# Layer 1 of a two-layer perceiver: the turn of the second rows between the products of q, k and of v, and a later start of the output bias

## The chip, the cores and the metric

The kernel runs on one core of one Trainium2 chip, all in float32. The metric is the device time of one execution in microseconds (us). TensorE (PE in the profile) multiplies, VectorE (DVE), ScalarE (ACT) and GpSimd (POOL) do the rest, SyncE (SP) issues the transfers. Each engine runs its own list of instructions in the written order; semaphores tie the lists together.

## The reference, cut to what matters

The input x has 64 batches of 32 rows of 512 values. Six blocks follow each other, each of the form x = x + f(layernorm(x)). Layer 0 has a cross attention, a self attention and a feed-forward step with adapters. Layer 1, the only part that the change touches, has these three:

```
x = x + mix(layernorm(x))                  # blend of crucial and other channels, gates from a convolution
h = layernorm(x);  q, k, v = split(h @ w_qkv.T + b_qkv)
p = softmax(where(causal, k q^T, -10000))  # 8 heads of 32
x = x + (p^T v) @ w_o.T + b_o              # b_o: the output bias
x = x + layernorm(x) @ (W * mask).T        # feed-forward
```

## The kernel before, in words

The 2048 rows are cut into 16 tiles of 128 rows (four batches each). Layer 1 takes every tile t through a list of stages. The ones that matter here, in the order of one tile:

- gate, add_rest, mix (DVE, lines 1809, 1816, 1822), turn_mix (four transposes on PE, line 1704), add_mix (DVE, line 1826: x = x + the turned mix).
- stats1, rstd1, rows1: the first norm. DVE takes the statistics (lines 1074 to 1079), POOL the power (line 1084), DVE writes the normalised rows to lane_xn (line 1089). turn1 transposes them on PE (line 1105), ACT copies the result to lane_xnT (line 1771).
- qkv on PE: 16 products of 128x128 for q and k (line 1716), then 4 products 128x256 for v (line 1720). ACT stores q and k (line 1778), DVE stores v (evac_v, line 1846), POOL spreads k over the batches (spread_k, line 1676).
- scores (PE, line 1728), mask (DVE, lines 1852 to 1857), shift (POOL, line 1684), exps (ACT, line 1783), turn_probs (DVE, lines 1863 to 1871), spread_p (ACT, line 1791), values (PE, line 1743), evac_ot (ACT, line 1797), project (PE, line 1751).
- bias (POOL, line 1671) adds b_o to x once rows1 of the tile has read x; add_proj (DVE, line 1876) adds the projection after it.
- stats2, rstd2, rows2, turn2, xnT2: the second norm, through the same helper lines as the first (1074 to 1105), so that line 1089 is rows1 or rows2, and line 1105 is turn1 or turn2.
- ffn (PE, line 1757), add_ffn (DVE, line 1880), store (SP).

Below, a number behind a stage is its tile: turn2(0) is the turn of tile 0's second rows.

Four tiles are under way at once, one in each of four lanes of buffers (t % 4). What an engine does in which order is set by a table: SLOTS1 gives every stage a time, in units of a tile's period, and over_lanes (line 1130 on) sorts all pairs of tile and stage by the tile's start plus the stage's slot. This is done three times: for an opening, with the starts of tiles 0 to 7 given in STARTS1 (0.00, 0.45, 0.99, 1.56, 3.50, 4.58, 5.35, 6.53); for a loop that runs twice and does four tiles each time, with starts one apart; and for a closing, with starts for tiles 12 to 15 (0.00, 37.47, 38.83, 39.38). The sort is the order of issue, no more: an engine comes to an instruction when all before it on this engine are issued, and waits there for its semaphores. On PE such a wait holds all products behind it.

Two waits are not obvious from the list. turn_mix(t) waits until add_ffn(t-4) has freed the lane. In places where PE would be idle for long, keep_busy (line 1518) puts products of a matrix of ones; in the closing there are seven of them (14 records of the trace) directly ahead of values(15).

Of the kernel before, what the change touches and what calls it, by code (L numbers as in the profile page):

```python
# [19 lines left out]
NT = B // TB  # L20
# [24 lines left out]
LANES = 4  # L45
# [1019 lines left out]
def norm_sems(sem, name):  # L1065

    return {k: sem(f"{name}_{k}") for k in ("stats", "veps", "rstd", "xn", "xt", "xnT")}
# [14 lines left out]
def norm_rstd(pool, n, t, u, small, neghalf):  # L1082
    pool.wait_ge(n["veps"], t + 1)
    pool.tensor_tensor(small["rstd"][:, u], small["veps"][:, u], neghalf[:], ALU.pow).then_inc(n["rstd"], 1)  # L1084
# [17 lines left out]
def norm_turn(pe, n, t, u, xn, out, ident):  # L1102
# [16 lines left out]
    "reduce_rest": 3.994,}  # L1119
SLOTS1 = {  # L1120
    "gate": 0.000, "add_rest": 0.027, "mix": 0.173, "turn_mix": 0.485, "add_mix": 0.614, "stats1": 0.707,
    "rstd1": 0.773, "rows1": 0.929, "bias": 2.020, "turn1": 1.011, "xnT1": 1.045, "qkv": 1.310,
    "evac_qk": 1.500, "evac_v": 1.762, "spread_k": 1.600, "scores": 2.006, "mask": 2.056, "shift": 2.136,
    "exps": 2.342, "turn_probs": 2.461, "spread_p": 2.571, "values": 2.919, "evac_ot": 2.919,
    "project": 3.015, "add_proj": 3.074, "stats2": 3.162, "rstd2": 3.245, "rows2": 3.395, "turn2": 3.470,
    "xnT2": 3.539, "ffn": 3.877, "add_ffn": 3.989, "store": 3.989,}

STARTS0 = ((0.00, 0.95, 1.89, 2.83, 3.83, 4.85, 5.82, 6.78),
# [386 lines left out]
def keep_busy(pe, out, ones, n):  # L1515

    for _ in range(n):
        pe.matmul(out[:, 0:P], ones[:], ones[:], start=True, stop=True)  # L1518
# [99 lines left out]
def layer1(nc, a, X, mask, ident, neghalf, x_tile, ps, bufs, blend, late, ones):  # L1618

    posT, Y, lanes, xn, xnT, small, jmask, _ = bufs  # L1620
    ctx = ExitStack()
    with ctx:
# [3 lines left out]
        def sem(name):  # L1626
            return ctx.enter_context(nc.semaphore(name))
# [8 lines left out]
        gate = sb("gate1", [P, 1])  # L1636

        n4, n5 = norm_sems(sem, "n4"), norm_sems(sem, "n5")
        names = ("gated", "gate_added", "mixed", "mix_turned", "mix_added", "bias_added", "qk_filled", "qkv_filled", "v_ready",
                 "qk_ready", "kd_ready", "s_filled", "s_kept", "s_masked", "max_done", "s_shifted", "p_ready",  # L1640
                 "sum_done", "rinv_ready", "p_turned", "pt_ready", "av_filled", "p_scaled",
                 "ot_ready", "proj_filled", "proj_added", "ffn_filled", "ffn_added")
        s = {k: sem(f"l1_{k}") for k in names}
        out_done = sem("out_done")

        mixed = lambda u: lanes[:, u, 0, 0:D]
# [8 lines left out]
        @block.sync  # L1655
        def _(sp):
            def store(t, u):
                sp.wait_ge(s["ffn_added"], t + 1)
                if isinstance(t, int):
                    sp.dma_start(a["y"][t], x_tile(t)).then_inc(out_done, 16)  # L1660
                else:
                    sp.dma_start(a["y"][bass.ds(t, 1)].rearrange("a p d -> (a p) d"), x_tile(t)).then_inc(out_done, 16)

            over_lanes(sp, SLOTS1, STARTS1, {"store": store})
            sp.wait_ge(out_done, 16 * NT)

        @block.gpsimd
        def _(pool):
            def bias_rows(t, u):
                pool.wait_ge(n4["xn"], t + 1)  # L1670
                pool.tensor_tensor(x_tile(t), x_tile(t), b_o[:], ALU.add).then_inc(s["bias_added"], 1)

            def spread_k(t, u):
                pool.wait_ge(s["qk_ready"], t + 1)
                for half in range(2):
                    ins = pool.tensor_tensor(Kd(u)[:, half], QK[:, u, 2 + half].rearrange("p (j k) -> p j k", j=TB)  # L1676
                                             .unsqueeze(2).to_broadcast([P, TB, 4, L]),
                                             jmask[:].unsqueeze(1).unsqueeze(3).to_broadcast([P, TB, 4, L]), ALU.mult)
                ins.then_inc(s["kd_ready"], 1)

            def shift(t, u):
                pool.wait_ge(s["max_done"], t + 1)
                v = p[:, u].rearrange("p (h k) -> p h k", h=EH)
                pool.tensor_tensor(v, v, small["rmax"][:, u, 0:EH].unsqueeze(2).to_broadcast([P, EH, L]), ALU.subtract)\
                    .then_inc(s["s_shifted"], 1)

            over_lanes(pool, SLOTS1, STARTS1, {
                "rstd1": lambda t, u: norm_rstd(pool, n4, t, u, small, neghalf),
                "bias": bias_rows, "spread_k": spread_k, "shift": shift,
                "rstd2": lambda t, u: norm_rstd(pool, n5, t, u, small, neghalf)})  # L1690

        @block.tensor
        def _(pe):
            def busy_until_first(t, n):

                if isinstance(t, int) and t == 0:
                    keep_busy(pe, high(LANES - 1), ones, n)

            def turn_mix(t, u):
                busy_until_first(t, 8)  # L1700
                pe.wait_ge(s["mixed"], t + 1)
                wait(pe, s["ffn_added"], t - LANES + 1)
                for c in range(DC):
                    mm = pe.transpose(low(u)[:, P * c:P * c + P], mixed(u)[:, P * c:P * c + P], ident[:])
                mm.then_inc(s["mix_turned"], 1)

            def turn1(t, u):
                busy_until_first(t, 10)
                norm_turn(pe, n4, t, u, xn, high(u), ident)

            def qkv(t, u):
                busy_until_first(t, 4)
                pe.wait_ge(n4["xnT"], t + 1)
                for n in range(4):
                    for c in range(DC):
                        mm = pe.matmul(low(u)[:, P * n:P * n + P], w_qkv[:, c, P * n:P * n + P], xnT[:, u, c],  # L1716
                                       start=(c == 0), stop=(c == DC - 1))
                mm.then_inc(s["qk_filled"], 1)
                for c in range(DC):
                    mm = pe.matmul(high(u)[:, 0:EW], xnT[:, u, c], w_qkv[:, c, 2 * EW:], start=(c == 0), stop=(c == DC - 1))  # L1720
                mm.then_inc(s["qkv_filled"], 1)

            def scores(t, u):
                pe.wait_ge(s["qk_ready"], t + 1)
                pe.wait_ge(s["kd_ready"], t + 1)
                for half in range(2):
                    for j in range(TB):
                        mm = pe.matmul(low(u)[L * j:L * j + L, P * half:P * half + P], QK[:, u, half, L * j:L * j + L],  # L1728
                                       Kd(u)[:, half, j], start=True, stop=True, tile_position=(0, L * j))
                mm.then_inc(s["s_filled"], 1)  # L1730

            def busy_at_end(t, n):

                if isinstance(t, int) and t >= NT - 2:
                    keep_busy(pe, high(0), ones, n[t - NT + 2])

            def values(t, u):
                busy_at_end(t, (0, 7))
                pe.wait_ge(s["pt_ready"], t + 1)
                pe.wait_ge(s["v_ready"], t + 1)  # L1740
                for h in range(EH):
                    n, at = h // 4, L * (h % 4)
                    mm = pe.matmul(high(u)[at:at + L, P * n:P * n + P], V[:, u, L * h:L * h + L],  # L1743
                                   pT(u)[:, P * h:P * h + P], start=True, stop=True, tile_position=(0, at))
                mm.then_inc(s["av_filled"], 1)

            def project(t, u):
                busy_at_end(t, (2, 0))
                pe.wait_ge(s["ot_ready"], t + 1)
                for n in range(EW // P):  # L1750
                    mm = pe.matmul(low(u), OT(u)[:, n], w_o[:, n], start=(n == 0), stop=(n == EW // P - 1))  # L1751
                mm.then_inc(s["proj_filled"], 1)

            def ffn(t, u):
                pe.wait_ge(n5["xnT"], t + 1)
                for c in range(DC):
                    mm = pe.matmul(low(u), xnT[:, u, c], w_ffn[:, c], start=(c == 0), stop=(c == DC - 1))  # L1757
                mm.then_inc(s["ffn_filled"], 1)

            over_lanes(pe, SLOTS1, STARTS1, {  # L1760
                "turn_mix": turn_mix, "turn1": turn1, "qkv": qkv,
                "scores": scores, "values": values, "project": project,
                "turn2": lambda t, u: norm_turn(pe, n5, t, u, xn, high(u), ident), "ffn": ffn})

# [39 lines left out]
        def _(dve):  # L1804
# [36 lines left out]
                return lambda t, u: norm_rows(dve, n, t, u, x_tile(t), small, xn)  # L1841

            def evac_v(t, u):
                dve.wait_ge(s["qkv_filled"], t + 1)
                wait(dve, s["av_filled"], t - LANES + 1)
                dve.tensor_tensor(V[:, u], high(u)[:, 0:EW], b_v[:], ALU.add).then_inc(s["v_ready"], 1)

# [126 lines left out]
```

## Time and profile before

| what | value |
| --- | --- |
| three runs, median (lowest to highest) | 2057.27 us (2054.42 to 2059.32) |
| profiled execution, its time | 2057.11 us |
| its span | 2055.3 us |
| granted clock of TensorE, mean | 0.994 |
| PE busy | 2000.9 us (97%) |
| DVE, POOL, ACT busy | 64%, 43%, 39% |
| layer 1, opening, 1812 to 1912 us | PE busy 89.01 of 100 us |
| layer 1, loop, 1912 to 2019 us | PE busy 104.85 of 107 us |
| layer 1, closing, 2019 to 2055 us | PE busy 29.31 of 36 us |

Times in the rows are in us from the start of the span. A row of the timeline has the start, the duration of the merged instructions (x8 is eight of them), the engine, the line, what is written and read, and in brackets how long the engine was idle before it and what ended this. A product in float32 is two records (x8 for four products). Ends on PE are modelled, so intervals from start to start are the safer measure there.

### The profile page before, as it was taken

Reading aid. Unit: us, or ns where it says so; the run is one execution under the profiler, and the core shown is the slowest. Engines: PE = TensorE matmul, PEld = TensorE weight load, DVE = VectorE, ACT = ScalarE, POOL = GpSimd, SP = SyncE. Lnnn points to the kernel's source line nnn. Section 1 sums busy time; section 2 is a strip of 40 time slices with the busy share of each in tenths; the row PEclk is TensorE's granted clock in tenths of the full one; section 3 lists DMA queues with packets and bytes.
Section 4 is the critical chain, followed back from the end, with each engine's and each line's share of the span. In section 5 each row is a group of like instructions: output and inputs, shape, how many; then the busy total and the mean of one; then the engine's idle time right before and its main releaser. Section 6 shows DMA issues by size and latency. Waiting matters only on the chain. (4 is left out here: it accounts for less than half of the span.)

```text
span 2055.3 us, 40252 instructions
## 1 busy us (share of the span) xinstructions
PE 2000.9 (97%) x12580; PEld 1634.0 (80%) x12580; DVE 1314.1 (64%) x4424; ACT 793.9 (39%) x2206; POOL 880.0 (43%) x1515
## 2 busy tenths in 40 slices
PE   9999999999999999999999999999899999888998
PEld 7989889898988989888898988988566666575775
DVE  5846648385574937558493764847476767667885
ACT  3444435344443434444343443534222232223332
POOL 5544636345453634545354363534233333223432
PEclk9999999999999999999999999999899999999999
DMA  7100001000000101001000100001100000000000
GB/s 291 42 26 26 31 15 32 24 31 25 25 31 15 41 15 33 23 25 31 24 32 15 34 21 25 31 18 72 47 1 1 1 0 0 31 1 21 17 21 26
DMA packets 28064, 62.77 MB, mean 31 GB/s; under 512 B 14257, under 2 KB 15473, under 8 KB 27042
## 3 DMA queue, kind: packets, MB, share of 16 engines
q1 hardware_dynamic: 27938, 61.46, 9.0%
q14 instruction: 92, 0.75, 0.1%
q8 instruction: 34, 0.56, 0.1%
HBM read 54.00 MB, written 4.29 MB: 28 GB/s over the span
## 5 line engine op out<-in xcount | busy, mean ns | idle before, releaser
L772 ACT ACTIVATE probs<-psLane,nmax 128x289 f32<-128x289 f32 x256 | 126.0, 497 | 469.9 <-DVE nmax L894 469.9
L934 DVE MAX8 top<-work 128x8 f32<-128x257 f32 x512 | 180.1, 413 | 2.7
L484 PE MATMUL psLane<-xnT,WqT 128*128 128x128 f32 x1536 | 179.5, 275 | 0.4 <-ACT QT L761 0.4
L484 PEld LDWEIGHTS psLane<-xnT,WqT 128*128 128x128 f32 x1536 | 176.9, 192 | 0.9 <-ACT QT L761 0.6
L919 DVE TENSOR_TENSOR X<-X,psLane 128x512 f32 (+1 forms) x16 | 11.0, 688 | 252.2 <-PE psLane L611 252.2
L611 PE MATMUL psLane<-WoT,OT 128*128 128x512 f32 x384 | 170.5, 601 | 1.4 <-DVE OT L914 1.4
L747 ACT ACTIVATE w_o<-psLane 128x384 f32<-128x384 f32 (+1 forms) x256 | 113.4, 450 | 90.4 <-PE psLane L537 89.3
L363 POOL TENSOR_TENSOR KT<-w_qkv 128x128 f32<-128x128 f32 x64 | 29.2, 456 | 273.1 <-ACT w_qkv L719 273.1
L557 PE MATMUL psLane<-KT,QT 96*128 96x289 f32 x512 | 146.0, 406 | 0.0
L611 PEld LDWEIGHTS psLane<-WoT,OT 128*128 128x128 f32 x384 | 73.6, 193 | 87.8 <-issue 86.1
L338 POOL TENSOR_TENSOR tails<-probs,unit 128x66 f32<-128x66 f32 x128 | 38.1, 298 | 242.8 <-ACT probs L772 208.5
L1084 POOL TENSOR_TENSOR lane_rstd<-lane_veps,neghalf 128x1 f32<-128x1 f32 x79 | 52.1, 659 | 168.0 <-DVE lane_veps L1079 168.0
L507 PE MATMUL psLane<-hid,WkT 128*128 128x256 f32 x512 | 122.7, 381 | 0.0
L891 DVE TENSOR_REDUCE rmax<-psLane 128x2 f32<-128x578 f32 x128 | 96.8, 756 | 34.0 <-PE psLane L557 33.8
L761 ACT ACTIVATE QT<-psLane 96x512 f32<-96x512 f32 x96 | 56.8, 592 | 154.0 <-PE psLane L484 153.4
L557 PEld LDWEIGHTS psLane<-KT,QT 96*128 96x128 f32 x512 | 90.8, 190 | 21.2 <-issue 7.2
L537 PE MATMUL psLane<-WvT,hid 128*128 128x192 f32 x512 | 104.2, 326 | 0.0
L537 PE MATMUL psLane<-w_ffn 128*128 128x192 f32 x512 | 104.1, 326 | 0.0
L914 DVE COPY OT<-psLane 128x384 f32<-128x384 f32 x64 | 34.9, 545 | 107.8 <-PE psLane L605 107.8
L580 PEld LDWEIGHTS psLane<-V,probsT 128*128 128x128 f32 x512 | 88.2, 190 | 18.0 <-issue 6.0
L938 DVE MATCH_REPLACE8 work<-top,work 128x257 f32<-128x257 f32 x256 | 102.2, 411 | 0.0
L938 DVE MATCH_REPLACE8 work<-top_last,work 128x257 f32<-128x257 f32 x256 | 102.2, 411 | 0.0
(244 smaller groups left out, 5140.7 us busy)
## 6 DMA issues: line engine op xcount, KB each, us to landing
hid<-in_ctxT SPq DMA_DIRECT2D x64, 514.0 KB, 3.5
y<-X SPq DMA_DIRECT2D x16, 256.0 KB, 2.0
X<-in_x SPq DMA_DIRECT2D x1, 3584.0 KB, 21.2
WqT<-in_WqT SPq DMA_DIRECT2D x4, 768.0 KB, 8.5
Vtail<-Vlat SPq DMA_DIRECT2D x128, 24.0 KB
WoT<-in_WoT SPq DMA_DIRECT2D x1, 3072.0 KB, 13.2
w_qkv<-in_w_qkv SPq DMA_DIRECT2D x2, 1536.0 KB, 6.9
w_ffn<-in_w_ffn SPq DMA_DIRECT2D x2, 1024.0 KB, 7.0
```

What stands on the lines that cost most here:

```text
L484: mm = pe.matmul(out[:, P * r:P * r + P], WqT[:, c, w:w + P], xnT[:, c, :], start=(c == 0), stop=(c == DC - 1))
L507: mm = pe.matmul(out[:, 0:MAIN], WkT[:, c, 2 * P:3 * P], hid[:, j, c, 0:MAIN], start=(c == 0), stop=(c == DC - 1))
L537: mm = pe.matmul(out, left(c), right(c), start=(c == 0), stop=(c == 1))
L557: mm = pe.matmul(psS[:, g % 2, 0:S], QT[:, g, j, :], KT[0:HD, j % 2, g, :], start=True, stop=True)
L580: pe.matmul(out, probsT[:, g % 2, 0, :], V[:, j % 2, 0, cols], start=(g % 2 == 0), stop=False)
L611: mm = pe.matmul(psM, OT[:, n // G, n % G].rearrange("p j q -> p (j q)"), WoT[:, n, :], start=(n == 0), stop=(n == NKT * G - 1))
L747: act.activation(vproducts[:, 2 * f:2 * f + n, :].rearrange("p a n -> p (a n)"), psKV[:, kv_bank(t, 7 * j + 3 + f), 0:VH * n], ACT.Copy).t ...
L761: ins = act.activation(QT[at:at + hi - lo, g].rearrange("p j (r q) -> p r j q", r=G), src[lo:hi], ACT.Copy)
L772: act.activation(probs[:, g, :], psS[:, g % 2, 0:S], ACT.Exp, bias=nmax[:, g:g + 1], scale=XSCALE, accum_out=rsum[:, j % 2, g:g + 1]).then ...
L891: dve.tensor_reduce(rmax[:, 2 * h:2 * h + 2], psS[:, :, 0:S], AX.X, ALU.max).then_inc(rmax_done, 1)
L934: ins = dve.max(top[step // 2][:, c, :], src[:, c, :] if step == 1 else work[:, c, :])
L938: ins = dve.match_replace(work[:, c, :], picked[:, c, :], src[:, c, :] if step == 2 else work[:, c, :], GONE)
```

## The change

The stage qkv becomes two stages, qk at slot 1.310 (where qkv was) and v at 1.420. The slot of turn2 falls from 3.470 to 3.405, so that in the loop turn2 of one tile comes between qk and v of another. And bias waits for the rows1 of the following tile, not of its own, for tiles 4 to 14; tiles 0 to 3 and 15 wait as before.

```
-    "rstd1": 0.773, "rows1": 0.929, "bias": 2.020, "turn1": 1.011, "xnT1": 1.045, "qkv": 1.310,
+    "rstd1": 0.773, "rows1": 0.929, "bias": 2.020, "turn1": 1.011, "xnT1": 1.045, "qk": 1.310, "v": 1.420,
...
-    "project": 3.015, ... "rows2": 3.395, "turn2": 3.470,
+    "project": 3.015, ... "rows2": 3.395, "turn2": 3.405,
...
             def bias_rows(t, u):
-                pool.wait_ge(n4["xn"], t + 1)
+                pool.wait_ge(n4["xn"], t + 2 if not isinstance(t, int) or LANES <= t < NT - 1 else t + 1)
...
-            def qkv(t, u):
+            def qk(t, u):
                 busy_until_first(t, 4)
                 pe.wait_ge(n4["xnT"], t + 1)
...
                 mm.then_inc(s["qk_filled"], 1)
+
+            def v(t, u):
                 for c in range(DC):
                     mm = pe.matmul(high(u)[:, 0:EW], xnT[:, u, c], w_qkv[:, c, 2 * EW:], start=(c == 0), stop=(c == DC - 1))
-                mm.then_inc(s["qkv_filled"], 1)
+                mm.then_inc(s["v_filled"], 1)
...
             def evac_v(t, u):
-                dve.wait_ge(s["qkv_filled"], t + 1)
+                dve.wait_ge(s["v_filled"], t + 1)
```

The number of instructions is the same on PE, DVE, ACT and SP, and only PE's order changes; POOL has one more register instruction in the loop. From line 1720 on the changed kernel's lines are two further (v is line 1722, scores 1730, values 1745, project 1753, ffn 1759).

First place, the opening on PE, from qk(3) on. Before, the two rows L1716 and L1720 are qkv(3), then come values(0), scores(2), project(0), values(1), project(1), turn2(0), scores(3), ffn(0), values(2) and turn2(1):

```order
L1716 MATMUL psLane<-lane_xnT,w_qkv 128x128 x16
L1720 MATMUL psLane<-w_qkv,lane_xnT 128x256 x4
L1743 MATMUL psLane<-lanes,lane_V 32x128 x8
L1728 MATMUL psLane<-lanes,lane_QK 32x128 x8
L1751 MATMUL psLane<-w_o,lane_xnT 128x512 x2
L1743 MATMUL psLane<-lanes,lane_V 32x128 x8
L1751 MATMUL psLane<-w_o,lane_xnT 128x512 x2
L1105 MATMUL psLane<-ident,lane_xn 128x128 x4
L1728 MATMUL psLane<-lanes,lane_QK 32x128 x8
L1757 MATMUL psLane<-w_ffn,lane_xnT 128x512 x4
L1743 MATMUL psLane<-lanes,lane_V 32x128 x8
L1105 MATMUL psLane<-ident,lane_xn 128x128 x4
```

Now the same stretch reads:

```order
L1716 MATMUL psLane<-lane_xnT,w_qkv 128x128 x16
L1745 MATMUL psLane<-lanes,lane_V 32x128 x8
L1722 MATMUL psLane<-w_qkv,lane_xnT 128x256 x4
L1730 MATMUL psLane<-lanes,lane_QK 32x128 x8
L1753 MATMUL psLane<-w_o,lane_xnT 128x512 x2
L1745 MATMUL psLane<-lanes,lane_V 32x128 x8
L1105 MATMUL psLane<-ident,lane_xn 128x128 x4
L1753 MATMUL psLane<-w_o,lane_xnT 128x512 x2
L1730 MATMUL psLane<-lanes,lane_QK 32x128 x8
L1105 MATMUL psLane<-ident,lane_xn 128x128 x4
L1759 MATMUL psLane<-w_ffn,lane_xnT 128x512 x4
L1745 MATMUL psLane<-lanes,lane_V 32x128 x8
```

values(0) now stands ahead of v(3), turn2(0) ahead of project(1), and turn2(1) ahead of ffn(0) and values(2); behind them both lists go on with turn_mix(4), project(2), ffn(1), turn2(2).

Second place, PE in the loop, one of its four tiles; before it is project, qk and v, turn2, turn_mix, ffn, values:

```order
L1751 MATMUL psLane<-w_o,lane_xnT 128x512 x2
L1716 MATMUL psLane<-lane_xnT,w_qkv 128x128 x16
L1720 MATMUL psLane<-w_qkv,lane_xnT 128x256 x4
L1105 MATMUL psLane<-ident,lane_xn 128x128 x4
L1701 REGISTER_ALU
L1704 MATMUL psLane<-ident,lanes 128x128 x4
L1757 MATMUL psLane<-w_ffn,lane_xnT 128x512 x4
L1743 MATMUL psLane<-lanes,lane_V 32x128 x8
```

Now:

```order
L1753 MATMUL psLane<-w_o,lane_xnT 128x512 x2
L1716 MATMUL psLane<-lane_xnT,w_qkv 128x128 x16
L1105 MATMUL psLane<-ident,lane_xn 128x128 x4
L1722 MATMUL psLane<-w_qkv,lane_xnT 128x256 x4
L1701 REGISTER_ALU
L1704 MATMUL psLane<-ident,lanes 128x128 x4
L1759 MATMUL psLane<-w_ffn,lane_xnT 128x512 x4
L1745 MATMUL psLane<-lanes,lane_V 32x128 x8
```

turn2 has moved ahead of v, so four products of v and turn_mix now lie between turn2 and the ffn of the same tile.

Third place, PE at the end, from project(14) on (L1518 is keep_busy; L1743 is values(15), the two L1105 are turn2(14) and turn2(15)). Before:

```order
L1751 MATMUL psLane<-w_o,lane_xnT 128x512 x2
L1518 MATMUL psLane<-ones 128x128 x7
L1743 MATMUL psLane<-lanes,lane_V 32x128 x8
L1105 MATMUL psLane<-ident,lane_xn 128x128 x4
L1751 MATMUL psLane<-w_o,lane_xnT 128x512 x2
L1757 MATMUL psLane<-w_ffn,lane_xnT 128x512 x4
```

Now:

```order
L1753 MATMUL psLane<-w_o,lane_xnT 128x512 x2
L1105 MATMUL psLane<-ident,lane_xn 128x128 x4
L1518 MATMUL psLane<-ones 128x128 x7
L1745 MATMUL psLane<-lanes,lane_V 32x128 x8
L1753 MATMUL psLane<-w_o,lane_xnT 128x512 x2
L1759 MATMUL psLane<-w_ffn,lane_xnT 128x512 x4
```

turn2(14) has moved ahead of the products of ones and of values(15).

## Rows read from the trace of the kernel before

**Rows 1.** Timeline of PE in the loop, one period of 13.44 us.
```profile
1948.09 3.70 PE L1757 MATMUL psLane<-w_ffn,lane_xnT 128*128 128x512 f32 x8 [0.25 <-ACT lane_xnT L1771]
1951.72 0.64 PE L1743 MATMUL psLane<-lanes,lane_V 128*32 128x128 f32 x16
...
1958.51 1.89 PE L1720 MATMUL psLane<-w_qkv,lane_xnT 128*128 128x256 f32 x8
1960.24 0.60 PE L1105 MATMUL psLane<-ident,lane_xn 128*128 128x128 f32 x4
1960.68 0.60 PE L1704 MATMUL psLane<-ident,lanes 128*128 128x128 f32 x4
1961.53 0.70 PE L1757 MATMUL psLane<-w_ffn,lane_xnT 128*128 128x512 f32 x1 [0.25 <-ACT lane_xnT L1771]
```

**Rows 2.** Timeline of DVE in the same period: rows1, add_ffn, gate, add_proj, rows2.
```profile
1950.48 1.48 DVE L1089 TENSOR_SCALAR lane_xn<-X,lane_mv,lane_rstd 128x512 f32 x1 [0.31 <-POOL lane_rstd L1084]
1951.88 0.67 DVE L1880 TENSOR_TENSOR X<-X,psLane 128x512 f32 x1
1952.48 0.68 DVE L1809 TENSOR_TENSOR lanes<-mask,blend 128x512 f32 x1
...
1955.15 0.69 DVE L1876 TENSOR_TENSOR X<-X,psLane 128x512 f32 x1
...
1958.06 0.55 DVE L1089 TENSOR_SCALAR lane_xn<-X,lane_mv,lane_rstd 128x512 f32 x1 [0.44 <-POOL lane_rstd L1084]
```

**Rows 3.** Timeline of POOL in the same period: the output bias.
```profile
1950.42 1.26 POOL L1671 TENSOR_TENSOR X<-X,b_o 128x512 f32 x1
```

**Rows 4.** Timeline of POOL and DVE in the opening: spread_k beside gate.
```profile
1896.63 2.48 POOL L1676 TENSOR_TENSOR lanes<-lane_QK,jmask 128x512 f32<-128x512 f32 x2 [0.49 <-ACT lane_QK L1778]
1896.97 1.25 DVE L1809 TENSOR_TENSOR lanes<-mask,blend 128x512 f32<-128x512 uint8 x1
```

**Rows 5.** Timeline of PE in the opening, values(1) to turn_mix(4).
```profile
1851.76 0.64 PE L1743 MATMUL psLane<-lanes,lane_V 128*32 128x128 f32 x16
1853.03 1.98 PE L1751 MATMUL psLane<-w_o,lane_xnT 128*128 128x512 f32 x4 [0.64 <-ACT lane_xnT L1797]
1856.59 0.66 PE L1105 MATMUL psLane<-ident,lane_xn 128*128 128x128 f32 x4 [1.57 <-DVE lane_xn L1089]
...
1857.93 3.70 PE L1757 MATMUL psLane<-w_ffn,lane_xnT 128*128 128x512 f32 x8
...
1863.49 0.66 PE L1105 MATMUL psLane<-ident,lane_xn 128*128 128x128 f32 x4 [1.29 <-DVE lane_xn L1089]
1864.18 0.63 PE L1704 MATMUL psLane<-ident,lanes 128*128 128x128 f32 x4
```

**Rows 6.** Timeline of DVE in the opening: add_proj(1) and rows2(1).
```profile
1858.53 0.68 DVE L1876 TENSOR_TENSOR X<-X,psLane 128x512 f32<-128x512 f32 x1
...
1862.60 0.84 DVE L1089 TENSOR_SCALAR lane_xn<-X,lane_mv,lane_rstd 128x512 f32<-128x512 f32 x1
```

**Rows 7.** Timeline of DVE in the opening: rows1(5), beside bias(4).
```profile
1887.09 1.50 DVE L1089 TENSOR_SCALAR lane_xn<-X,lane_mv,lane_rstd 128x512 f32<-128x512 f32 x1
```

**Rows 8.** Timeline of PE in the closing: ones, turn2(14), project(15), ffn(14), turn2(15).
```profile
2037.77 1.72 PE L1518 MATMUL psLane<-ones 128*128 128x128 f32 x14
...
2041.07 0.66 PE L1105 MATMUL psLane<-ident,lane_xn 128*128 128x128 f32 x4 [0.75 <-DVE lane_xn L1089]
2041.56 1.88 PE L1751 MATMUL psLane<-w_o,lane_xnT 128*128 128x512 f32 x4
2043.28 3.60 PE L1757 MATMUL psLane<-w_ffn,lane_xnT 128*128 128x512 f32 x8
2046.71 0.60 PE L1105 MATMUL psLane<-ident,lane_xn 128*128 128x128 f32 x4
```

**Rows 9.** PE at the end of layer 0: its timeline.
```profile
1793.89 1.11 PE L1105 MATMUL psLane<-ident,lane_xn 128*128 128x128 f32 x4 [4.00 <-DVE lane_xn L1089]
```

**Rows 10.** Windows: stretch, busy us of PE, PEld, DVE, ACT, POOL, granted clock, DMA share, GB/s.
```profile
1794.00:1799.00 5.00, 5.00 (x24) 4.97 (x24) 4.90 (x9) 0.60 (x1) 1.27 (x1) 0.50 0.00 0
```

More of the change, by code:

```diff
@@ L1121 @@
     "gate": 0.000, "add_rest": 0.027, "mix": 0.173, "turn_mix": 0.485, "add_mix": 0.614, "stats1": 0.707,
-    "rstd1": 0.773, "rows1": 0.929, "bias": 2.020, "turn1": 1.011, "xnT1": 1.045, "qkv": 1.310,
+    "rstd1": 0.773, "rows1": 0.929, "bias": 2.020, "turn1": 1.011, "xnT1": 1.045, "qk": 1.310, "v": 1.420,
     "evac_qk": 1.500, "evac_v": 1.762, "spread_k": 1.600, "scores": 2.006, "mask": 2.056, "shift": 2.136,
     "exps": 2.342, "turn_probs": 2.461, "spread_p": 2.571, "values": 2.919, "evac_ot": 2.919,
-    "project": 3.015, "add_proj": 3.074, "stats2": 3.162, "rstd2": 3.245, "rows2": 3.395, "turn2": 3.470,
+    "project": 3.015, "add_proj": 3.074, "stats2": 3.162, "rstd2": 3.245, "rows2": 3.395, "turn2": 3.405,
     "xnT2": 3.539, "ffn": 3.877, "add_ffn": 3.989, "store": 3.989,}
@@ L1638, in layer1 @@
         n4, n5 = norm_sems(sem, "n4"), norm_sems(sem, "n5")
-        names = ("gated", "gate_added", "mixed", "mix_turned", "mix_added", "bias_added", "qk_filled", "qkv_filled", "v_ready",
+        names = ("gated", "gate_added", "mixed", "mix_turned", "mix_added", "bias_added", "qk_filled", "v_filled", "v_ready",
                  "qk_ready", "kd_ready", "s_filled", "s_kept", "s_masked", "max_done", "s_shifted", "p_ready",
@@ L1760, in _ @@
             over_lanes(pe, SLOTS1, STARTS1, {
-                "turn_mix": turn_mix, "turn1": turn1, "qkv": qkv,
+                "turn_mix": turn_mix, "turn1": turn1, "qk": qk, "v": v,
                 "scores": scores, "values": values, "project": project,
```

## The prediction

> **What bounds the kernel now.** I read the page first: TensorE (PE) is busy 97% of the span, no other engine over 64%. The change touches layer 1 alone, so I took the windows of its three parts: the loop of 107 us leaves PE 2 us of idle time, the opening 11 of 100 us, the closing 7 of 36 us (table above). Then the timeline, engine by engine, for who ends each of PE's waits.
>
> In the loop a period is 13.44 us, from one ffn to the next, and PE has one bubble in it [rows 1]. Four transposes take 0.44 us from start to start (turn2, 1960.24 to 1960.68), but ffn follows turn_mix after 0.85 us: 0.41 us too late, since ACT's copy of turn2's result is not done. The ffn behind a bubble also takes 0.20 us longer: 3.63 us to the next start [rows 1] against 3.43 us behind other products [rows 8]. So 0.61 us per tile, 4.9 us over the loop's 8 tiles, is all that the loop can give.
>
> In the opening and in the closing PE is not the bound: PE waits there for DVE's rows [rows 5, 8]. There it matters what stands behind a waiting turn, because PE holds it too.
>
> **The loop, 8 tiles.** turn2 goes ahead of v. ACT then has v (1.73 us) and turn_mix to cover its copy, and the bubble goes. What is late next is turn2 itself: rows2 ends at 1958.06 + 0.55 = 1958.61 [rows 2], 0.10 us after v started, which is where turn2 now wants to start [rows 1]. So I follow DVE round once, counted from the start of turn_mix. In the period shown this start is 1960.68 - 13.44 = 1947.24.
>
> rows1 starts at +3.24 and takes 1.48 us beside the bias, 0.55 us alone [rows 2]. With the new wait it is alone and ends at +3.79; bias starts a semaphore later, +3.87, and ends at +5.13 (1.26 us, [rows 3]). That relief alone is worth nothing: add_ffn waits for PE. ffn now starts at +0.46 and add_ffn at about +4.10 (3.60 us and a semaphore); gate is due 0.60 us after it, at +4.70, in the middle of the moved bias.
>
> Does the bias hold gate up? Beside spread_k, gate took 1.25 us instead of 0.68 [rows 4]; rows1 beside the bias ended at 1951.96, 0.28 us after the bias (1951.68) [rows 2, 3]. Both look like an instruction that starts to stream only when POOL's is over. I take gate as held until +5.13 and done 0.54 us later, +5.67, against +5.38 if free. From gate's end to add_proj are 1955.15 - 1953.16 = 1.99 us [rows 2]: +7.66, against +7.91 before. From there rows2 ends 3.46 us later, +11.12; turn2 starts at +11.17, and v follows a turn that waited 0.49 us later [rows 8], +11.66. With 1.73 us of v the next turn_mix starts at 13.39. The period falls by 0.05 us: the bubble before ffn has become a wait of turn2 of about 0.5 us. Eight tiles: **-0.4 us**. Bounds: with no wait anywhere -0.57 a tile (-4.6); with bias a little later, so that it holds add_rest too, +0.2 a tile (+1.6). I take the value near nothing because the ring through DVE closes at nearly the old period.
>
> The Trainium skill, page "SBUF — State Buffer", section "Who interferes with whom", states the same as a rule: a DVE instruction with two inputs in SBUF, or a two-port copy or tensor_scalar, and a GpSimd instruction share a port pair, and the one that comes second is blocked until the first is over. By it the bias is only moved from rows1 onto gate, whose mask and blend both lie in SBUF; a free gate would make the loop's term about -2.3 us instead. By that rule, the trace agrees with its 1.25 us [rows 4] and 1.48 us [rows 2].
>
> **The opening.** First turn2(0) ahead of project(1). Before, project(1) ran at 1853.03, while turn2(0) waited until 1856.59 [rows 5]. Now PE idles from the end of values(1), 1852.40, to turn2(0), which may come 0.6 us earlier (values(0) ahead of v(3) lets ACT and spread_k(3) go sooner): 1855.98. project(1) ends near 1858.45. That is hidden: add_proj(1) was at 1858.53 anyhow, behind DVE's own work [rows 6]. So rows2(1) still ends at 1863.44 [rows 6], and turn2(1) stays at 1863.49.
>
> Then turn2(1) ahead of ffn(0). Before, ffn(0) and values(2) ran from 1857.93, in the shadow of the wait for rows2(1) [rows 5]. Now they start behind it: ffn(0) at 1863.49 + 0.49 = 1863.98, add_ffn(0) 3.64 us later at 1867.62, done and signalled 0.72 us later. turn_mix(4), which waits for it, starts at 1868.34 instead of 1864.18 [rows 5]: **+4.2 us**. Nothing gives that back: project(2), add_proj(2), rows2(2) and turn2(2) hang on each other behind turn_mix(4), and the later waits of the opening end on DVE work that follows from them.
>
> Against it stands bias(4), which no longer lies on rows1(5): 1.50 us [rows 7] becomes 0.55, with some 0.15 given back where bias(4) now meets the mask of scores. This is on the path through mask, exps and turn_probs to the next rows: **-0.8 us** (0 to -0.95).
>
> **The closing.** turn2(14) is ahead of the ones and of values(15). rows2(14) comes no sooner, so turn2 stays at 2041.07; but then the ones (0.49 later, 1.72 us long), values(15) and ACT's copy, with 1.14 to 1.27 us from values to project (1851.76 to 1853.03 is 1.27, [rows 5]), come before project(15): about 2044.5 instead of 2041.56 [rows 8]. ffn(14), turn2(15) and ffn(15) follow it in one chain: **+2.9 us** (2.8 to 3.0).
>
> **The clock.** The change makes three long gaps on PE: 1852.40 to 1855.98 (3.6 us), about 1859.0 to 1863.49 (4.5), and, with the ones no longer in it, 2037.8 to 2041.07 (3.2). Before, the longest gap of layer 1's opening was 1.57 us at full clock [rows 5], while after a gap of 4.00 us [rows 9] the five microseconds that follow show a granted clock of 0.50, the lower level of 1.2 GHz [rows 10]. There 24 records took 5.00 us; at full clock 14 took 1.72 [rows 8], so 24 would take 2.95: a fall costs 2.05 us of PE time. The gap of 4.5 us should bring one; those of 3.2 and 3.6 us lie between the two rows, nearer to 4.00. I take two falls in all, one in the opening and one in the closing: **+4.1 us** (0 to 7).
>
> **Sum.** -0.4 + 4.2 - 0.8 + 2.9 + 4.1 = +10.0 us on the profiled execution's 2057.11 us, 2067.1. That execution was 0.16 us under the median of the runs, so the median comes to 2067.3 us.
>
> **Rivals.** (1) The clock stays up: all else as above, +5.9, 2063.2 us. For it: a gap's effect can depend on where it falls, and 3.2 and 3.6 us are in no row. Against: 4.00 us did it.
> (2) Heavier: three falls, one of them on project(1), which then pushes add_proj(1) and rows2(1) by over 1 us, and a loop at its upper bound: +13 to +15, 2071 us.
> (3) The other side: gate is not held, turn2's rows are ready when qk ends, and the loop gives its whole 4.6 us, while the opening's 4.2 us vanish in PE waits that follow anyway. The point that decides is whether rows2 ends before qk does. Then -4.6 + 1 + 2.9 = -0.7, 2056.6 us. For it: rows2 misses v's start by 0.10 us only. Against: [rows 4], and the later waits hang on the delayed tile.
> (4) The change does nothing that can be seen, because the waits trade places everywhere: 2057 us. Against it speaks that two of the three places have no cover at all.
>
> **Chances.** The forecast with two falls, 50%; (1) 24%; (2) 9%; (3) 12%; (4) 5%. A measurement of this kernel can tell about 0.2%, 4.1 us, from no change. Faster by more than that needs (3) with the closing spared: 4%. Within it: the rest of (3), (4) and a part of (1), 15%. Slower 81%. The range holds (1), the forecast and the lower part of (2): 2060 to 2071.5 us; the forecast's own range is 2064 to 2070.
>
> **What would show it.** In the profile after: PE idle some 4.5 us before turn2(1), with line 1084 or 1089 as its releaser, and turn_mix(4) 4 us or more behind its old place; granted clock under 1.00 in the opening and behind 2041; the loop's period 13.3 to 13.5 us, with no wait of ffn and one of 0.3 to 0.6 us ahead of turn2, rows1 at 0.55 us, gate at 1.1 to 1.25 us; project(15) 3 us after turn2(14). I am wrong if the loop's period is under 13.2 us (gate free), if the opening's end moves by under 2 us, or if the closing doesn't grow.

## The result, and the profile after

| | before | after |
| --- | --- | --- |
| median of six runs each | 2055.99 us | 2065.31 us |
| lowest to highest | 2053.8 to 2059.32 | 2063.84 to 2073.18 |
| ratio, 95% interval | | 1.0048 [1.0029, 1.0067] |

The changed kernel is 9.3 us slower; 10.0 was predicted. The execution that was profiled is the longest of its six (2073.18 us, span 2071.4, mean granted clock 0.988; the other spans are 2062.0 to 2064.7 at 0.992 to 0.994). It shows the places well, but the clock's share larger than usual. The windows of its layer 1 (columns as in [rows 10]; the closing now runs past 2055 us, so that the third window holds only its first part):

```profile
1812.00:1912.00 100.00, 84.69 (x605) 60.57 (x606) 64.92 (x156) 27.23 (x69) 32.98 (x35) 0.95 0.03 12
1912.00:2019.00 107.00, 104.14 (x759) 73.56 (x758) 82.37 (x204) 37.99 (x96) 43.60 (x48) 1.00 0.06 20
2019.00:2055.00 36.00, 30.70 (x214) 21.33 (x212) 19.66 (x51) 11.04 (x28) 10.81 (x13) 0.92 0.04 15
```

The granted clock is below 1.00 in the opening and in the closing, not in the loop. In the opening, PE's timeline (against [rows 5]) reads from values(1) to turn_mix(4):

```profile
1852.80 0.65 PE L1745 MATMUL psLane<-lanes,lane_V 128*32 128x128 f32 x16
1857.12 0.66 PE L1105 MATMUL psLane<-ident,lane_xn 128*128 128x128 f32 x4 [3.68 <-DVE lane_xn L1089]
1857.61 3.23 PE L1753 MATMUL psLane<-w_o,lane_xnT 128*128 128x512 f32 x4
...
1865.85 1.11 PE L1105 MATMUL psLane<-ident,lane_xn 128*128 128x128 f32 x4 [4.15 <-DVE lane_xn L1089]
1866.76 6.03 PE L1759 MATMUL psLane<-w_ffn,lane_xnT 128*128 128x512 f32 x8
1872.72 0.64 PE L1745 MATMUL psLane<-lanes,lane_V 128*32 128x128 f32 x16
1873.67 0.63 PE L1704 MATMUL psLane<-ident,lanes 128*128 128x128 f32 x4 [0.30 <-DVE X L1882]
```

PE now stands still behind two waiting turns, turn2(0) and turn2(1), and what follows each gap takes over one and a half times as long: project(1) 3.23 us instead of 1.98, ffn(0) 6.03 instead of 3.70. In the loop (against [rows 1]) PE has, from one ffn to the next:

```profile
1957.02 3.60 PE L1759 MATMUL psLane<-w_ffn,lane_xnT 128*128 128x512 f32 x8
...
1967.89 0.66 PE L1105 MATMUL psLane<-ident,lane_xn 128*128 128x128 f32 x4 [0.38 <-DVE lane_xn L1089]
1968.38 1.89 PE L1722 MATMUL psLane<-w_qkv,lane_xnT 128*128 128x256 f32 x8
1970.11 0.60 PE L1704 MATMUL psLane<-ident,lanes 128*128 128x128 f32 x4
1970.55 3.60 PE L1759 MATMUL psLane<-w_ffn,lane_xnT 128*128 128x512 f32 x8
```

The wait ahead of ffn is gone and one ahead of turn2 has come; the period is 1970.55 - 1957.02 = 13.53 us. Beside it DVE (against [rows 2]), and the bias on POOL (against [rows 3]):

```profile
1959.83 0.55 DVE L1089 TENSOR_SCALAR lane_xn<-X,lane_mv,lane_rstd 128x512 f32 x1 [0.31 <-POOL lane_rstd L1084]
1960.66 0.69 DVE L1882 TENSOR_TENSOR X<-X,psLane 128x512 f32 x1 [0.28 <-PE psLane L1759]
1961.26 1.13 DVE L1811 TENSOR_TENSOR lanes<-mask,blend 128x512 f32 x1
```

```profile
1960.56 1.28 POOL L1671 TENSOR_TENSOR X<-X,b_o 128x512 f32 x1 [0.77 <-DVE lane_xn L1089]
```

rows1 takes 0.55 us instead of 1.48, and gate 1.13 instead of 0.68: the bias is off the one and on the other. In the closing (against [rows 8]) PE shows turn2(14), ones, values(15), project(15), ffn(14):

```profile
2050.12 1.11 PE L1105 MATMUL psLane<-ident,lane_xn 128*128 128x128 f32 x4 [3.13 <-DVE lane_xn L1089]
2051.02 3.19 PE L1518 MATMUL psLane<-ones 128*128 128x128 f32 x14
2054.15 1.08 PE L1745 MATMUL psLane<-lanes,lane_V 128*32 128x128 f32 x16
2055.73 3.78 PE L1753 MATMUL psLane<-w_o,lane_xnT 128*128 128x512 f32 x4 [0.50 <-ACT lane_xnT L1799]
2059.31 3.64 PE L1759 MATMUL psLane<-w_ffn,lane_xnT 128*128 128x512 f32 x8
```

project(15) starts 5.61 us behind turn2(14), where it started 0.49 us behind it [rows 8].

Where the 16.1 us between the two profiled spans (2071.4 and 2055.3) lie, from start to start of the same stages in both timelines:

| stretch | longer by |
| --- | --- |
| ahead of layer 1's first turn_mix (unchanged work) | 0.85 us |
| from there to turn_mix(4) | 8.64 us |
| turn_mix(4) to the scores at the loop's entry | -0.93 us |
| the loop to the values at its end | 0.49 us |
| from there to ffn(15) | 7.02 us |

Of the 8.64 us, 8.45 lie between values(1) and turn_mix(4) (1873.67 - 1852.80 = 20.87 us against 12.42 [rows 5]). With the same stretches at full clock as the measure (experiment 4), 4.26 us of them are the price of the order; 1.33 us are the slow project(1), which brings turn2(1) 13.05 us behind values(1) instead of 11.72; and 2.86 us are the slow turn2(1) and ffn(0), from turn2(1) to turn_mix(4) 7.82 us instead of 4.96. The 7.02 us are 2.91 of order (turn2(14) to ffn(15) takes 9.84 us in experiment 4 and 6.93 before) and 4.11 of clock. The opening has one more change of order than the three places named above: ffn(2) at 1887.05 now stands ahead of v(4) at 1890.49. It costs nothing that shows: from turn_mix(4) to the scores at the loop's entry it is 46.67 us here and 46.69 us in experiment 1, where v(4) is first.

### The profile page after: what moved, and what is told of

The parts are those of the page before. It is cut to its first block and busy times, and to the rows that moved or that the text cites. A ratio compares the mean times of both kernels' runs of the same rounds, so it can differ in the third digit from the quotient of the medians.

```text
span 2071.4 us, 40254 instructions
## 1 busy us (share of the span) xinstructions
PE 2009.4 (97%) x12580; PEld 1638.5 (79%) x12580; DVE 1309.4 (63%) x4424; ACT 794.2 (38%) x2206; POOL 880.3 (42%) x1515
```

## The experiments

Each was timed in five rounds against the kernel before on the same chip. Differences are between medians, with the ratio's interval beside them. Where a kernel has its own order at the ends, a small table gives the slot of single tiles there, and nothing else.

**1. The old order at both ends** (label e1_ends_old): the changed kernel, but in the opening and the closing PE's order is that of before.

```
+OPENING_SLOTS1 = {(n, t): x for n, x in (("turn2", 3.470), ("v", 1.3101)) for t in range(2 * LANES)}
+LATE_SLOTS1 = {("turn2", NT - 2): 3.470}
```

> The changed kernel with the order of before in the opening and in the closing; the loop and the wait of the bias as changed. Theory (the loss is in the two ends, from what a waiting turn holds behind it): +0.5 us in the loop and -0.9 us for bias(4) remain, so 2055 to 2056 us, the same as before, and no fall of the clock in layer 1. Rival (the loss comes from the loop and from the bias's wait, which delays DVE's gate): the run stays near the changed kernel, 2062 us or more.

Measured: 2053.95 against 2054.68 us, ratio 0.9998 [0.9989, 1.0007]; period 13.53 us. The expectation was 2055 to 2056 us; the result is 1 us under it. The loop and the bias together cost and give nothing that can be told; all of the loss sits in the ends.

**2. The opening alone** (e2_opening_alone): the kernel before, with the changed order in the opening only.

```
+OPENING_SLOTS1 = {(n, t): x for n, x in (("turn2", 3.405), ("v", 1.420)) for t in range(2 * LANES)}
```

> The kernel before with the changed order in the opening alone (v a stage of its own, turn2 at 3.405, there only); loop, closing and the wait of the bias as before. Theory: +4.2 us behind turn2(1) at full clock, and 0 to 4.5 us more by falls of the clock in the two gaps: 2060 to 2064 us, turn_mix(4) at least 4.1 us later. Rival (the opening's waits are given back later, since PE waits there anyway): within 1 us of before.

Measured: 2062.31 against 2054.68 us, +7.6, ratio 1.0038 [1.0024, 1.0051]. The gaps (3.68 us ahead of turn2(0), 4.43 ahead of turn2(1)) and what follows them are much like those of the changed kernel. project(1), then turn2(1) and ffn(0):

```profile
1859.16 3.41 PE L1757 MATMUL psLane<-w_o,lane_xnT 128*128 128x512 f32 x4
...
1867.58 1.11 PE L1105 MATMUL psLane<-ident,lane_xn 128*128 128x128 f32 x4 [4.43 <-DVE lane_xn L1089]
1868.48 5.58 PE L1763 MATMUL psLane<-w_ffn,lane_xnT 128*128 128x512 f32 x8
```

**3. The closing alone** (e3_closing_alone): the kernel before, with turn2(14) ahead of the ones and values(15).

```
+LATE_SLOTS1 = {("turn2", NT - 2): 3.405}
```

> The kernel before with turn2(14) ahead of the ones and of values(15), and nothing else. Theory: +2.9 us at full clock, up to 4 us more if the clock falls in the gap of 3.1 us: 2059 to 2062 us; project(15) 3.2 to 3.6 us behind turn2(14) at full clock, over 5 us at half. Rival (the earlier copy of turn2's result speeds ffn(14), which hides it): within 1 us of before.

Measured: 2059.03 against 2054.68 us, +4.4, ratio 1.0022 [1.0012, 1.0031]. In its profile turn2(14) comes at 2040.24 behind a gap of 3.13 us, the ones take 3.19 us (half clock), and project(15) starts 4.90 us behind turn2(14). The three parts, -0.7 + 7.6 + 4.4 = +11.3 us, add up to the whole change's 9.3 within their intervals, which are 2 to 4 us wide to either side.

**4. Filling the gaps** (e5_ones): the changed kernel, with products of ones (they work for nothing but the clock) ahead of the three turns.

```
+            def turn2(t, u):
+                ones_ahead = {0: 12, 1: 16, NT - 2: 11}
+                if isinstance(t, int) and t in ones_ahead:
+                    keep_busy(pe, high(u), ones, ones_ahead[t])
+                norm_turn(pe, n5, t, u, xn, high(u), ident)
```

> The changed kernel with products of ones ahead of turn2(0) (12), turn2(1) (16) and turn2(14) (11), which fill the three long gaps of PE. Theory (a part of the loss is half clock behind these gaps): the granted clock stays at 1.00 all through layer 1, the time falls by 1 to 4 us to about 2061 to 2063 us, and what is left over before is about 6 us: +4.2, -0.9, +0.5, +2.9. Rival (the slow rows of the profiled execution are rare, the loss is all waiting): the time stays at 2065 us.

Measured: 2060.97 against 2054.68 us, +6.3, ratio 1.0029 [1.0016, 1.0042]. That is 3 us less than the changed kernel, though it does more work. The opening, and turn2(14), ones and project(15) of the closing:

```profile
1848.86 0.64 PE L1745 MATMUL psLane<-lanes,lane_V 128*32 128x128 f32 x16
1849.43 2.94 PE L1518 MATMUL psLane<-ones 128*128 128x128 f32 x24
1853.20 0.66 PE L1105 MATMUL psLane<-ident,lane_xn 128*128 128x128 f32 x4 [0.82 <-DVE lane_xn L1089]
...
1861.07 3.60 PE L1765 MATMUL psLane<-w_ffn,lane_xnT 128*128 128x512 f32 x8
1865.54 0.63 PE L1704 MATMUL psLane<-ident,lanes 128*128 128x128 f32 x4 [0.30 <-DVE X L1888]
...
2042.00 0.66 PE L1105 MATMUL psLane<-ident,lane_xn 128*128 128x128 f32 x4 [0.68 <-DVE lane_xn L1089]
2042.49 1.73 PE L1518 MATMUL psLane<-ones 128*128 128x128 f32 x14
2045.30 1.98 PE L1753 MATMUL psLane<-w_o,lane_xnT 128*128 128x512 f32 x4 [0.50 <-ACT lane_xnT L1805]
```

And its windows:

```profile
1820.00:1900.00 80.00, 74.55 (x555) 54.26 (x554) 52.22 (x124) 24.45 (x64) 30.24 (x33) 1.00 0.04 14
1900.00:2050.00 150.00, 143.79 (x1042) 100.63 (x1041) 106.80 (x270) 49.95 (x126) 56.90 (x63) 1.00 0.05 18
```

At full clock throughout, values(1) to turn_mix(4) takes 1865.54 - 1848.86 = 16.68 us against 1864.18 - 1851.76 = 12.42 [rows 5], +4.26; turn2(14) to project(15) takes 3.30 against 0.49 [rows 8], +2.81. So this kernel holds the price of the order alone, and the changed kernel's remainder is the clock. The timed executions, sorted by their mean granted clock, say the same without the profiles. At 0.992 the changed kernel's spans are 2064.2 and 2064.7 us, and those of the kernel before 2057.2 to 2057.8; at 0.993 they are 2062.4 and 2062.8 against 2055.2 to 2056.9. This kernel has four executions at 0.996, 2058.9 us in the mean, against 2051.9 for the kernel before at the same clock. So both stand some 7 us above the kernel before at equal clock, near the 6.6 us that the terms of the order, the bias and the loop add up to. What sets them apart in the median is the clock.

**5. turn2(1) back** (e6_turn1_back): the changed kernel, turn2(1) alone behind ffn(0) and values(2) again.

```
+OPENING_SLOTS1 = {("turn2", 1): 3.470}
```

> The changed kernel with turn2(1) alone put back behind ffn(0) and values(2); turn2(0) stays ahead of project(1). Theory (turn2(0) is covered by DVE's own work at full clock, turn2(1) is what costs): 4.2 us and a fall of the clock less, 2059 to 2061 us; turn_mix(4) within 1 us of its place in the kernel before, if the gap ahead of turn2(0) brings no fall. Rival (turn2(0) ahead of project(1) is what starts the loss): less than 1.5 us faster than the changed kernel.

Measured: 2060.19 against 2054.42 us, +5.8, ratio 1.0024 [1.0014, 1.0034]: some 3.5 us less than the changed kernel. The gap ahead of turn2(0) is still there, and in the profile the half clock comes with it. From values(1) to turn_mix(4):

```profile
1850.13 0.64 PE L1749 MATMUL psLane<-lanes,lane_V 128*32 128x128 f32 x16
1854.45 0.66 PE L1105 MATMUL psLane<-ident,lane_xn 128*128 128x128 f32 x4 [3.68 <-DVE lane_xn L1089]
1854.94 3.55 PE L1757 MATMUL psLane<-w_o,lane_xnT 128*128 128x512 f32 x4
1858.43 0.65 PE L1734 MATMUL psLane<-lanes,lane_QK 128*32 128x128 f32 x16
...
1863.50 0.66 PE L1105 MATMUL psLane<-ident,lane_xn 128*128 128x128 f32 x4 [0.23 <-DVE lane_xn L1089]
1864.19 0.63 PE L1708 MATMUL psLane<-ident,lanes 128*128 128x128 f32 x4
```

turn_mix(4) starts at 1864.19 us, but this is its place in the kernel before (1864.18) only by chance, since layer 1 starts 1.83 us earlier in this execution. The stretch is 14.06 us against 12.42 [rows 5], +1.64. The slow project(1) accounts for all of it: 3.49 us from its start to the next, where experiment 4 has 1.81. So with turn2(1) back, nothing is left of the 4.26 us of order.

In the closing of the same execution a gap of 3.13 us, as long as the changed kernel's, brings no half clock: the ones behind it take 1.73 us, not 3.19.

```profile
2040.63 0.66 PE L1105 MATMUL psLane<-ident,lane_xn 128*128 128x128 f32 x4 [3.13 <-DVE lane_xn L1089]
2041.12 1.73 PE L1522 MATMUL psLane<-ones 128*128 128x128 f32 x14
```

**6. The old bias wait** (e4_bias_old): the changed kernel, but bias waits for its own tile's rows again.

```
-                pool.wait_ge(n4["xn"], t + 2 if not isinstance(t, int) or LANES <= t < NT - 1 else t + 1)
+                pool.wait_ge(n4["xn"], t + 1)
```

> The changed kernel with the bias waiting for its own tile's rows again. Theory (the bias's wait is worth a little: it frees rows1(5), and holds gate for less than it frees rows1): rows1 back at 1.48 us in the loop, gate at 0.68, add_ffn held by rows1 to about +4.64 from turn_mix, period about 13.6 us instead of 13.53, and 0.9 us more in the opening: 1 to 2.5 us slower than the changed kernel, about 2067 us. Rival (the bias on gate is what makes turn2 wait): period 13.2 us, 2 us faster than the changed kernel, 2063 us.

Measured: 2069.71 against 2054.42 us, +15.3, ratio 1.0073 [1.0058, 1.0087]. rows1 is back at 1.48 us, gate at 0.68, the turn's wait grows from 0.38 to 0.50 us, and the period to 13.65 us. So the new wait helps the changed order. In the profiles that is some 0.9 us over the loop and 0.9 at rows1(5) (turn_mix(4) to the loop's scores takes 47.61 us instead of 46.67). The medians' excess over the changed kernel is 6 us. A part of it is the clock: at a mean granted clock of 0.992 three spans of this kernel are 2066.1, 2067.0 and 2068.8 us, 2.9 us above the changed kernel's 2064.2 and 2064.7 in the mean. Three further executions of this kernel are at 0.990 and 0.991, while of the changed kernel's six only the profiled one is under 0.992. The two ratios' intervals are 3 to 4 us wide to either side, so the excess itself is not known well.

**7. The bias wait alone** (e9_bias_wait_alone): the kernel before with only that line changed the other way.

> The kernel before with the changed wait of the bias alone, no order changed. Theory (the bias moves from rows1 onto gate; where turn2 is not early, this is no loss): rows1 0.55 us, gate about 1.1 us in the loop, period unchanged at 13.44 us since ffn still waits for ACT's copy, and 0.9 us less in the opening from rows1(5): 2053.5 to 2054 us, within the noise. Rival (the gate that is held delays add_proj and with it everything): 1.5 us slower or more, 2056 us.

Measured: 2053.9 against 2054.4 us, ratio 0.9991 [0.9982, 1.0000]; period 13.44, ffn still waits for ACT. The expectation for gate missed: it takes 0.68 us, not 1.1. POOL and DVE show why:

```profile
1977.80 1.28 POOL L1671 TENSOR_TENSOR X<-X,b_o 128x512 f32 x1 [0.77 <-DVE lane_xn L1089]
```

```profile
1979.10 0.68 DVE L1809 TENSOR_TENSOR lanes<-mask,blend 128x512 f32 x1
```

The bubble ahead of ffn and the slow ffn behind it put gate later, 5.28 us behind turn_mix instead of 4.67, so that bias, which ends at 1979.08, is just over. In the steady loop the two meet only with the new order; at the loop's entry they meet here too, and the one gate there (1911.58) takes 1.20 us.

**8. The bias out of DVE's way** (e7_bias_after_shift): both ends as before, turn2 between qk and v in the loop, and there the bias behind shift on POOL.

```
-    ... "bias": 2.020,
+    ... "bias": 2.150,
...
-                pool.wait_ge(n4["xn"], t + 2 if not isinstance(t, int) or LANES <= t < NT - 1 else t + 1)
+                pool.wait_ge(n4["xn"], t + 2 if isinstance(t, int) and LANES <= t < NT - 1 else t + 1)
```

> The ends ordered as before, turn2 between qk and v in the loop, and the bias in the loop behind shift (slot 2.150) with the wait for its own tile's rows, where DVE adds the projection and takes statistics. Theory (gate held by the bias is what leaves a wait of turn2): rows1 0.55 us and gate 0.68 us at once, add_proj bound by PE, turn2 waits 0.1 to 0.2 us, period 13.15 us; 8 times 0.38 us less than with the bias ahead of gate: 2 to 3 us faster than before, 2052 us. Rival (the bias holds something else there, rstd2 or the statistics): period 13.4 us or more, 2054 to 2055 us.

Measured: 2052.16 against 2054.42 us, -2.3, ratio 0.9987 [0.9978, 0.9996]. Now rows1 (0.55) and gate (0.69) are both free, and the period is mostly 13.24 us (13.17 to 13.40). What is late next is rows2, since its rstd2 on POOL takes 0.97 us beside DVE's mix:

```profile
1966.62 0.97 POOL L1084 TENSOR_TENSOR lane_rstd<-lane_veps,neghalf 128x1 f32<-128x1 f32 x1
```

**9. And mix behind rows2** (e8_bias_mix): the same, with mix behind rows2 in the loop.

```
-    ... "mix": 0.173,
+    ... "mix": 0.430,
```

> As the kernel before it (bias behind shift), and in the loop mix goes behind rows2 on DVE (slot 0.430). Theory (mix ahead of rows2 costs rstd2 0.42 us, and this is the last wait of turn2): rstd2 0.55 us instead of 0.97, rows2 before qk ends, no wait on PE in the loop, period 12.87 us: 4.5 to 5 us faster than before, 2050 us. Rival (mix then pushes turn_probs into spread_k, which holds it about 1 us): period 13.1 us or more, no faster than the kernel without this step.

Measured: 2048.80 against 2054.42 us, ratio 0.9975 [0.9964, 0.9987], **5.6 us faster than before** and the best of all. PE, then POOL and DVE in its loop:

```profile
1961.28 3.73 PE L1720 MATMUL psLane<-lane_xnT,w_qkv 128*128 128x128 f32 x32
1964.85 0.60 PE L1105 MATMUL psLane<-ident,lane_xn 128*128 128x128 f32 x4
1965.29 1.89 PE L1726 MATMUL psLane<-w_qkv,lane_xnT 128*128 128x256 f32 x8
1967.02 0.60 PE L1708 MATMUL psLane<-ident,lanes 128*128 128x128 f32 x4
1967.45 3.60 PE L1763 MATMUL psLane<-w_ffn,lane_xnT 128*128 128x512 f32 x8
```

```profile
1963.51 0.55 POOL L1084 TENSOR_TENSOR lane_rstd<-lane_veps,neghalf 128x1 f32<-128x1 f32 x1
1964.09 0.55 DVE L1089 TENSOR_SCALAR lane_xn<-X,lane_mv,lane_rstd 128x512 f32 x1 [0.66 <-POOL lane_rstd L1084]
```

rows2 ends at 1964.64, 0.21 us before turn2 starts at 1964.85. The period is 12.93 us (13.08 once, where the loop's second run begins), and the window of the loop shows PE busy without a break:

```profile
1912.00:2012.00 100.00, 100.00 (x730) 71.29 (x729) 76.16 (x197) 37.41 (x95) 37.52 (x46) 1.00 0.06 20
```

**10. The turn back behind v** (e10_turn_back): that kernel, with turn2 behind v in the loop as before.

```
-    ... "qk": 1.310, "v": 1.420, ... "turn2": 3.405,
+    ... "qk": 1.310, "v": 1.3101, ... "turn2": 3.470,
```

> The fastest kernel so far (bias behind shift, mix behind rows2) with turn2 back behind v in the loop too. Theory (turn2 between qk and v is worth the bubble ahead of ffn, once its rows are ready): the bubble of 0.41 us and the slow first ffn come back, period 13.44 us, 8 times 0.5 us slower than with turn2 ahead: 2053 us, 0.5 to 1.5 us under before. Rival (the gain came from DVE and POOL being freed, the turn's place is worth nothing): 2049 to 2050 us.

Measured: 2053.99 against 2054.40 us, ratio 1.0000 [0.9991, 1.0009]; the period is 13.44 again, and ffn waits for ACT:

```profile
1957.76 3.70 PE L1763 MATMUL psLane<-w_ffn,lane_xnT 128*128 128x512 f32 x8 [0.25 <-ACT lane_xnT L1777]
```

So the turn between qk and v is worth 5.2 us in the medians and 4.3 in the two profiles (the periods together), but only once its rows are there; earlier rows alone are worth nothing that can be told.

## Why the prediction was right

**The opening, +4.2 us: right.** At full clock the same stretch is 4.26 us longer (experiment 4). turn2(1) alone carries it: with it back, only what the slow project(1) costs is left (experiment 5). That project(1) behind turn2(0) is hidden held only at full clock, where turn2(1) starts 11.72 us behind values(1), as before; at half clock it delayed turn2(1) by 1.3 us, as rival 2 had it.

**The closing, +2.9 us: right.** 2.81 us to project(15) and 2.91 to ffn(15) at full clock (experiment 4). The 5.61 us of the profiled execution are this and the half clock.

**bias(4), -0.8 us: right.** rows1(5) took 0.54 us instead of 1.50 [rows 7], and the stretch from turn_mix(4) to the loop is 0.93 us shorter. It follows the bias's wait and not the order: 46.69 us with the new wait and the old order (experiment 1), 47.61 with the old wait and the new order (experiment 6), 47.60 before.

**The loop, -0.4 us: the mechanism right, the sign off.** The period rose by 0.09 us instead of falling by 0.05, +0.5 us over the measured stretch. ffn's wait went, turn2's came (0.38 us; 0.3 to 0.6 announced), rows1 takes 0.55, gate 1.13. The step that was mis-sized is "bias starts a semaphore later": counted as 0.08 us, it was 1960.56 - 1960.38 = 0.18 us. With gate done only after the bias, it goes round the ring: gate ends 5.80 us behind turn_mix instead of the 5.67 worked out, and from there each stage followed as worked out (1.99 us to add_proj, 3.46 to the end of rows2). That gate is held by the bias is shown by both sides: 1.13 us where they meet, 0.68 and 0.69 us where the bias has ended (experiment 7) or was moved (8). In the first case it then ends 0.55 us after the bias, much as estimated (0.54). The Trainium skill says in "SBUF — State Buffer", section "Who interferes with whom", that the second of the two to come is blocked until the first is over; the trace agrees, since gate ends at 1962.39 and the bias at 1961.84. One sum beside the forecast was off: by the prediction's own chain a gate free from the start gives a period of 13.39 - 0.29 = 13.10 us and a term of -2.7 us, not -2.3.

**The clock, +4.1 us: right that it falls, the size not.** In the profiled execution half clock is seen behind three gaps, not two, and is worth 4.2 us in the opening and 4.1 in the closing, twice the two falls of 2.05. Over the runs its price is the changed kernel's 9.3 us less the 6.3 us of the kernel with its gaps filled, 3 us. That kernel's ones came at no visible price, but were not timed by themselves, so the 3 us have both intervals on them (about 4 to either side). By the terms at full clock, 4.26 + 2.81 - 0.93 + 0.5 = 6.6 us, the clock's part is 2.7 us, and with the 7 us of the comparison at equal clock (experiment 4) it is 2.3 us.

**The sum, +10.0 against +9.3 us: partly luck.** The loop came out 0.9 us above its term and the clock 1 to 1.5 us below, and the two cancel. +9.3 stands nearer to the forecast than to rival 1's +5.9 with no fall at all, but its interval begins at +6.0 us, so that the time alone hardly tells it from rival 1. The half clock in the profiled execution does, and the mean granted clocks do: 0.988 to 0.994 here, against 0.994 to 0.997 in experiment 4.

**The other side (rival 3) fell,** both halves of it: the loop gave nothing and the opening's 4.2 us were not given back. But its deciding point was the right one. Once rows2 ended before qk (experiment 9), the loop gave what it could: in the profile 4.3 us over its periods, where 4.6 had been put as the most. The other 0.9 us of that kernel's gain in the profile are rows1(5) in the opening.

**Still open:** why the kernel with the old bias wait on the changed order is granted less clock, and so comes out 6 us slower in the median rather than 1.8, and which gaps bring a fall of the clock. A gap of 3.13 us ahead of turn2(14) was followed by half clock in the changed kernel and in experiments 3 and 6, but by full clock in experiment 5.

## What to carry to other kernels

An engine that takes its list in order pays for an early wait with everything behind it: move a waiting instruction forward only where its input is already there, and judge the start and the end of a pipeline apart from its loop, since the same slot that is near nothing in the loop cost 7 us at the ends. A wait that is moved off one instruction should be followed to the one it lands on: the bias went from rows1 to gate, and only a third place, free of both, and mix moved as well, let the turn's move pay in full. A gap on TensorE can have a second price beside its length, half clock behind it. Products of ones in the gaps kept the clock at 1.00 here and bought back some 3 us, a figure with a wide interval.

## What was not expected of the hardware

- A semaphore from DVE to a waiting tensor_tensor of POOL took 0.18 us (rows1's end at 1960.38, bias at 1960.56); the way back is shorter (rstd2's end on POOL at 1964.06, rows2 on DVE at 1964.09, experiment 9).
- DVE also holds POOL: a 128x1 rstd took 0.97 us beside DVE's mix and 0.55 us without it, and that instruction decided when PE could turn the rows.
- The clock's price differs between runs of one program: the changed kernel's spans run from 2062.0 us at a mean granted clock of 0.994 to 2071.4 us at 0.988, and those of the kernel before, in the experiments, from 2050.5 at 0.996 to 2058.1 at 0.994.
